# Cross-attention and an eight-expert layer on one core: a new layout of the first two periods, and a new order of ScalarE's and VectorE's work in all of them

## The reference

```
h = layernorm(x)
q = h @ wq;  k = ctx @ wk;  v = ctx @ wv            # 16 heads of 64
x2 = x + softmax(q k^T / 8) v @ wo + bo
g = layernorm(x2)
gates = softmax(g @ router_w + router_b)            # 8 experts, the best 2 are chosen
# each expert takes its first 640 tokens in order of token number
x_out = x2 + sum over chosen e: gate_e * (gelu(g @ w1[e] + b1[e]) @ w2[e] + b2[e])
```

## Time and profile before

| | |
|---|---|
| median of 3 runs | 1056.79 us (1056.28 to 1056.82) |
| the profiled execution's own time | 1054.35 us |
| its span, first to last instruction | 1052.5 us |
| PE, DVE, ACT, POOL busy | 968.4, 774.7, 628.0, 260.1 us |
| mean granted TensorE clock | 0.977 of full speed |

### The profile page before, as it was taken

The page is one execution under the profiler, slowest core; times in us unless marked ns, Lnnn a source line. Parts: engine busy times, 40 slices in busy tenths (PEclk is TensorE's granted clock), DMA queues, the critical chain, the costliest instruction groups (busy, mean ns, idle before and its releaser), DMA issues.

```text
span 1052.5 us, 22859 instructions
## 1 busy us (share of the span) xinstructions
PE 968.4 (92%) x8224; PEld 872.0 (83%) x8224; DVE 774.7 (74%) x2096; ACT 628.0 (60%) x1738; POOL 260.1 (25%) x428
## 2 busy tenths in 40 slices
PE   4789999999999999999999999999845999999996
PEld 3678888888888888888888888888644999999996
DVE  4777778788887878788787878878663667766662
ACT  3777777766776767677766767777522334443330
POOL 2320211223131322313132231301231322222332
PEclk9899999999999999999999999999976999999998
DMA  8530101000010101011010101000024244445522
GB/s 226 149 105 2 32 1 32 22 31 23 31 51 7 39 13 31 13 31 42 2 41 6 31 8 32 16 1 15 12 97 172 60 93 124 125 125 132 132 26 26
DMA packets 47822, 56.73 MB, mean 54 GB/s; under 512 B 5228, under 2 KB 43098, under 8 KB 47584
## 3 DMA queue, kind: packets, MB, share of 16 engines
q1 hardware_dynamic: 38880, 46.30, 14.2%
q0 software_dynamic: 8832, 8.98, 5.3%
HBM read 36.01 MB, written 24.20 MB: 57 GB/s over the span
## 4 chain that ended last, share of the span: by engine, by line
PE 70%; ACT 12%; DVE 8%; issue 6%; DMA 1%; POOL 1%; POOLq 0%; another core or an unknown queue 0%; SPq 0%; ACTq 0%; DVEq 0%
PE psum L494 33%; PE psum L678 11%; PE psum L587 10%; PE psum L557 8%; PE psum L573 7%; ACT prob L739 6%; ACT probt L693 3%; DVE prob L907 3%; ACT kh L693 1%; PE psum L643 1%; DVE kl L844 1%; PE psum L605 1%; DVE negmax L896 1%; DMA slot_table<-row,picki 1%; ACT ah L693 1%
## 5 line engine op out<-in xcount | busy, mean ns | idle before, releaser
L739 ACT ACTIVATE prob<-psum,negmax 128x256 f32<-128x256 f32 x512 | 241.5, 489 | 98.2 <-DVE negmax L896 98.2
L693 ACT ACTIVATE probt<-psum 128x512 f32<-128x512 f32 x256 | 160.1, 631 | 41.2 <-PE psum L573 40.1
L896 DVE TENSOR_REDUCE negmax<-psum 128x2 f32<-128x512 f32 x256 | 159.0, 683 | 22.8 <-PE psum L557 22.4
L907 DVE TENSOR_SCALAR prob<-prob,invtot 128x256 f32<-128x256 f32 x512 | 160.2, 376 | 4.5
L573 PE MATMUL psum<-ident,prob 128*128 128x128 f32 x1024 | 153.2, 273 | 1.8 <-ACT probt L693 1.0
L820 ACT ACTIVATE hid<-psum,b1t 128x640 f32<-128x640 f32 x64 | 50.9, 796 | 136.3 <-PE psum L494 136.3
L573 PEld LDWEIGHTS psum<-ident,prob 128*128 128x128 f32 x1024 | 119.6, 142 | 13.9 <-issue 3.8
L587 PE MATMUL psum<-probt,v 128*64 128x256 f32 x1024 | 126.0, 389 | 0.0
L446 POOL DMA_INDIRECT slot_table<-row,picki x64 | 65.8, 1028 | 198.6 <-DVE picki L1009 171.8
L739 ACT ACTIVATION_READ_ACCUMULATOR prob<-psum,negmax 128x1 f32 x512 | 112.8, 220 | 0.0
L557 PE MATMUL psum<-kh,qh 64*128 64x256 f32 x512 | 84.1, 307 | 30.2 <-ACT probt L693 26.4
(11 more groups left out here) (155 smaller groups left out, 2738.8 us busy)
## 6 DMA issues: line engine op xcount, KB each, us to landing
w1r<-in_w SPq DMA_DIRECT2D x8, 1024.0 KB, 8.1
w2r<-in_w SPq DMA_DIRECT2D x8, 1024.0 KB
slot_table<-blank SPq DMA_DIRECT2D x8, 662.5 KB, 9.7
rows<-slot_table SPq DMA_DIRECT2D x8, 662.5 KB, 5.3
xin<-in_x SPq DMA_DIRECT2D x16, 256.0 KB, 2.9
out_rows<-x SPq DMA_DIRECT2D x16, 256.0 KB, 3.2
c<-in_ctxt SPq DMA_DIRECT2D x16, 128.0 KB, 3.0
c<-in_ctxt SPq DMA_DIRECT2D x32, 64.0 KB, 2.9
```

Source lines behind the costliest of these rows:

```text
L693: copy = lambda dst, src, **kw: act.activation(dst, src, ACT.Copy, **kw)
L739: last = act.activation(prob[:, m % 2, u, qb, :], psum[:, u, qb * S:(qb + 1) * S], ACT.Exp, bias=negmax[:, m % 2, u, qb:qb + 1], accum_out ...
L896: dve.tensor_reduce(negmax[:, m % 2, u, :], psum[:, u, :].rearrange("p (q s) -> p q s", q=ST), AX.X, ALU.max, negate=True).then_inc(sem("m ...
L907: last = dve.tensor_scalar(prob[:, m % 2, u, qb, :], prob[:, m % 2, u, qb, :], invtot[:, m % 2, u, qb:qb + 1], None, ALU.mult)
```

## The change

The first two periods get their own order in `timeline()`, ahead of a loop that now starts at m = 1. TensorE turns the unit matrix 28 times ahead of the first `xt` and 8 times behind it, into a PSUM bank that nobody reads then (`warm`). wq and wk come in two quarters of 256 columns and a half (`SPLITS`); wv and wo come in halves and are split by GpSimd alone (`vsplit`, a cast and a subtraction of 1024 columns). The q of period 1 is made ahead of the scores of period 0. The constants and the sums with the output's bias stand later on GpSimd (`constants` in period 2, `residual` for batches 0 and 1 in period 3), and so does the clearing of the table.

In every period: ScalarE does `exp1` right behind `exp0`, ahead of `pv`'s head; its copy of v (`v_sb`) goes behind the copy of `turn2`. On VectorE the ranks, and the addition that makes x2 from the second half of the output projection (`x2add`), go from the end of r = 0 into r = 1, between `max1` and `max2`.

At the end: w1 and w2 of expert 0 load once q is complete and x2 of batch 13 is stored; ScalarE makes the heads at the end of period 63 (`whi`) and VectorE the rests at four places of the last stages (`wlo`). The weights of expert 1 load ahead of the wait for the last scatter. The first expert's rows come in three DMAs with a semaphore each, and the first half of `up` starts with two groups of rows. In the last batch, two additions to `before` that nobody reads are left out.

```diff
-SPLITS = [(0, 0), (1, 0), (2, 0), (0, 1), (1, 1), (2, 1), (3, 0), (3, 1)]
+SPLITS = [(0, 0, 256), (1, 0, 256), (0, 256, 512), (1, 256, 512), (0, 512, 1024), (1, 512, 1024)]
+VSPLITS = [(2, 0, 512), (2, 512, 1024), (3, 0, 512), (3, 512, 1024)]
...
-    out = [("ln1_stats", 0), ("ctx", 0), ("split", 0), ("ln1", 0), ("split", 1), ("xt", 0), ("q", 0), ("k", 0),
-           ("split", 2), ("split", 3)]
-    for m in range(PERIODS + 1):
+    out = [("ln1_stats", 0), ("ctx", 0), ("ln1", 0), ("split", 0), ("split", 1), ("warm", 0), ("xt", 0), ("warm", 1),
+           ("split", 2), ("split", 3), ("q", 0), ("k", 0), ("q", 1), ("vsplit", 0), ("vsplit", 1), ("hi", 4),
+           ("scores", 0), ("max0", 0), ("max1", 0), ("max2", 0), ("max3", 0), ("exp0", 0), ("k", 1), ("exp1", 0),
+           ("lo", 4), ("exp2", 0), ("exp3", 0), ("v", 0), ("v_sb", 0), ("hi", 5), ("inv0", 0), ("norm0", 0),
+           ("norm1", 0), ("ctx", 1)]
+    for m in range(1, PERIODS + 1):
...
-        out += [("scores", m), ("max0", m), ("max1", m), ("max2", m), ("max3", m), ("exp0", m)] if live else []
+        out += [("scores", m), ("max0", m), ("max1", m), ("exp0", m), ("exp1", m)] if live else []
+        if r == 1 and 3 <= b < B:
+            out += [("rank", b - 3)]
+        if r == 1 and 2 <= b < B:
+            out += [("x2add", ST * (b - 2) + 1)]
+        out += [("lo", 5)] if m == 1 else []
+        out += [("max2", m), ("max3", m)] if live else []
...
-            out += [("ln2_stats", B - 2), *scaled]
+            out += [("ln2_stats", B - 2), *scaled, ("wlo", 0)]
...
-        out += [("exp1", m)] if live else []
...
+        out += [("ln1_stats", 1)] if m == 1 else []
...
-        out += {0: [("split", 4)], 1: [("split", 5)], 2: [("split", 6)], 3: [("split", 7)]}.get(m, [])
...
-            out += {0: [("ln1_stats", 1)], 1: [("ln1", 1)]}.get(r, [])
+            out += {1: [("vsplit", 2), ("ln1", 1)], 2: [("vsplit", 3), ("constants", 0)],
+                    3: [("residual", 0), ("residual", 1)]}.get(r, [])
...
-            out += {0: [("gate", b - 3), ("rank", b - 3)], 3: [("pick", b - 3)]}.get(r, [])
+            out += {0: [("gate", b - 3)], 3: [("pick", b - 3)]}.get(r, [])
...
         out += [("turn2", m - 1)] if turned else []
+        out += [("v_sb", m)] if live else []
...
+            out += [("whi", piece) for piece in range(WSPLITS)]
...
-    out += [("slot", last - 2), ("ln2", last - 1), ("keys", last - 2), ("pick", last - 2),
+    out += [("slot", last - 2), ("ln2", last - 1), ("keys", last - 2), ("pick", last - 2), ("wlo", 1),
...
-            ("gate", last - 1), ("o", ST * B - 2), ("rank", last - 1), ("o", ST * B - 1), ("ln2_stats", last),
-            ("pos", last - 1), ("slot", last - 1), ("keys", last - 1), ("pick", last - 1), ("ln2", last)]
+            ("gate", last - 1), ("wlo", 2), ("o", ST * B - 2), ("x2add", ST * B - 2), ("rank", last - 1), ("o", ST * B - 1),
+            ("x2add", ST * B - 1), ("ln2_stats", last),
+            ("pos", last - 1), ("slot", last - 1), ("keys", last - 1), ("pick", last - 1), ("ln2", last), ("wlo", 3)]
...
             load_x(0)
+            load_split(0)
             load_ctx(0)
...
+            for at in range(1, 4):
+                load_split(at)
+            load_vsplit(0)
+            load_split(4)
+            load_split(5)
             load_x(1)
             load_ctx(1)
...
+            load_vsplit(1)
+            sp.dma_start(bo_all[:, :], bo.partition_broadcast(P)).then_inc(sem("const_in"), 16)
+            load_vsplit(2)
+            load_vsplit(3)
             load_x(2)
             load_x(3)
...
+            load_ctx(2)
             sp.wait_ge(sem("blank"), 1)
...
+                if b == B - 3:
+                    sp.wait_ge(sem("q"), PERIODS)
+                    load_w(0)
...
+            load_w(1)
             sp.wait_ge(sem("scatter"), 16 * 2 * ST * B)
             all_stored(sp)
             load_rows(0)
             sp.dma_start(b2_all[:, :, :], b2.partition_broadcast(P)).then_inc(sem("b2_in"), 16)
             load_rows(1)
-            for e in range(1, NE):
+            load_rows(2)
+            for e in range(2, NE):
...
+                    for u in range(TURNS):
+                        s0, s1 = 2 * u, min(2 * u + 2, ET)
+                        sp.dma_start(rows[:, 0, s0:s1, :],
+                                     table[s0 * P:s1 * P, :].rearrange("(s p) w -> p s w", p=P))\
+                          .then_inc(sem(f"rows_first{u}"), 16)
...
+            def vsplit(w):
+                pool.wait_ge(sem(f"v_in{w}"), 48 if VSPLITS[w][0] == 2 else 16)
+                whole, head, rest_ = vpieces(w)
+                link(pool.tensor_copy(head, whole))
+                pool.tensor_tensor(rest_, whole, head.bitcast(F32), ALU.subtract).then_inc(sem("vsplit"), 1)
...
+            def warm(at):
+                for j in range((28, 8)[at]):
+                    pe.transpose(psum[:, 4, j % 4 * P:(j % 4 + 1) * P], ident[:, :], ident[:, :])
...
-                pe.wait_ge(sem("buf_lo"), TURNS * (e + 1))
+                pe.wait_ge(sem("buf_lo"), TURNS * (e + 1) - (e == 0))
...
+                        if at == 0 and half == 1:
+                            pe.wait_ge(sem("buf_lo"), TURNS)
...
             def keys(b):
                 dve.wait_ge(sem("slots"), b + 1)
-                for t in range(ST):
+                for t in range(ST if b + 1 < B else 0):
```

More of the change, by code:

```diff
@@ L118, in timeline @@
         if m == PERIODS - 1:
-            out += [("gate", b - 2), ("rank", b - 2), ("o", ST * (b - 1) + 1), ("pos", b - 2)]
+            out += [("gate", b - 2), ("rank", b - 2), ("o", ST * (b - 1) + 1), ("x2add", ST * (b - 1) + 1),
+                    ("pos", b - 2)]
+            out += [("whi", piece) for piece in range(WSPLITS)]
         if r == 1 and 3 <= b < B:
@@ L268, in all_stored, with rows_ready @@
                 eng.wait_ge(sem(f"x2_out{r}"), 16 * B // 2)
+        def rows_ready(eng, e, u):
+            if e == 0:
+                eng.wait_ge(sem(f"rows_first{u}"), 16)
+            else:
+                eng.wait_ge(sem(f"rows_in{e % 2}"), 16 * ((e + 1) // 2))
         @block.sync
@@ L457, in _ @@
                     inverse_root(stage[:3], n)
-                if stage == "ln1":
-                    if n == 1 and "c" not in did:
-                        did.add("c")
-                        constants()
-                    ln1(n)
+                if stage == "vsplit":
+                    vsplit(n)
+                if stage == "constants":
+                    constants()
+                if stage == "residual":
+                    residual(n)
                 if stage == "pick":
@@ L535, in v_ @@
                 if n in (0, 2):
-                    pe.wait_ge(sem("split_lo"), 3 if n == 0 else 6)
+                    pe.wait_ge(sem("vsplit"), 1 if n == 0 else 2)
                 cols, tt = slice(half * 512, half * 512 + 512), slice(t * P, (t + 1) * P)
@@ L756, in pv @@
                 if m == PER_B:
-                    act.wait_ge(sem("split_lo"), 8)
+                    act.wait_ge(sem("vsplit"), 4)
                 if b >= 2:
@@ L772, in gate @@
                 act.activation(lexp[:, :, :], logit[:, :, :], ACT.Exp).then_inc(sem("gate_exp"), 1)
-            steps = dict(split=split, xt=xt, q=q, k=k, v=v_, pv=pv, x2t=x2t_, gate=gate,
-                         exp0=lambda m: exps(m, 0), exp1=lambda m: exps(m, 1), exp2=lambda m: exps(m, 2),
-                         exp3=lambda m: exps(m, 3), turn0=lambda m: turn(m, 0), turn1=lambda m: turn(m, 1),
-                         turn2=lambda m: turn(m, 2), turn3=lambda m: turn(m, 3))
-            for stage, n in TIMELINE:
-                if stage in steps:
-                    steps[stage](n)
             def split_w(e, piece):
                 r, part, cut = e % 2, *divmod(piece, WSPLITS // 2)
+                if e == 0:
+                    act.wait_ge(sem(("k", "v")[part]), (PERIODS, 4 * B)[part])
                 act.wait_ge(sem(("w1_in", "w2_in")[part]), 16 * (e + 1))
@@ L793, in split_w @@
                     .then_inc(sem("wsplit_hi"), 1)
+            steps = dict(split=split, hi=split, xt=xt, q=q, k=k, v_sb=v_, pv=pv, x2t=x2t_, gate=gate,
+                         whi=lambda piece: split_w(0, piece),
+                         exp0=lambda m: exps(m, 0), exp1=lambda m: exps(m, 1), exp2=lambda m: exps(m, 2),
+                         exp3=lambda m: exps(m, 3), turn0=lambda m: turn(m, 0), turn1=lambda m: turn(m, 1),
+                         turn2=lambda m: turn(m, 2), turn3=lambda m: turn(m, 3))
+            for stage, n in TIMELINE:
+                if stage in steps:
+                    steps[stage](n)
             def turn_rows(e, u):
@@ L1059, in weigh @@
                                   None, ALU.mult).then_inc(sem("y"), 1)
-            for piece in range(WSPLITS):
-                split_w(0, piece)
             for u in range(TURNS):
```

133 lines of the change are left out of this document (63 added, 70 removed).

## The result

The changed kernel took 1027.17 us (median of 4 runs, 1025.74 to 1029.63) beside 1056.53 of the kernel before: a ratio of 0.9725, 95% interval 0.9705 to 0.9745, 2.7% faster. 1025 was forecast. The profiled execution took 1026.53 us with a span of 1024.8, 27.7 less than the 1052.5 of before; 31.8 had been forecast for it.

The account below looks back on a forecast made before the run. TensorE, busy for 92% of the span, was taken as the bound. Steady periods 14, beginning 14.8 and end 3 sum to 31.8 us, off the profiled 1054.35: 1022.5, plus 2.44 for the median: 1025; range 1014 to 1037.

Parts of the forecast that it names:

- Beginning: Start up to the ninth scores: new order and layout bring them from 109.80 to 95.0, 14.8 us gained, bounds 7 and 20.
- floor of 9.33 a period: Steady periods: TensorE's own work when nothing waits, 9.33 us together; periods 3 to 7 of the start were counted at it.
- Steady periods: From the ninth scores on: reordered VectorE and ScalarE work removes the waits before the scores, 14 us gained, bounds 5 and 16.
- the loss in r=2: Period r=2 of each batch: late exps cost 0.15 us a batch, taken 13 times off the 16.1 us of waits.
- exp1 ahead of `ah` costs nothing: ScalarE in the steady periods: both exps end with the product (3.5 against 3.58 us), so moving exp1 costs nothing.
- r=2 holds 2.87+0.44 more TensorE work, which covers it: Period r=2: exps start 2.7 us behind their scores, and the extra TensorE work of 2.87+0.44 us hides that.
- rival D: Periods with a late second maximum: exp1 ahead of `ah` delays it and q's copy, 51 us, total 1090; chance 0.03.
- End: End of attention up to the experts: scatter, additions, first rows and first product gain 3 us, bounds 0.5 and 4.5.
- priced at -0.5: Splits of expert 0's weights beside the scatter of 758: may cost 1.0 us on the chain, half of it taken.
- E: Start: GpSimd's pieces take 8 us each, table clear at 80, a VectorE copy waits 6 us more: 1031; chance 0.06.
- A: Slow start: port lock or late clock keeps 8 us of the beginning's gain away: 1033; chance 0.18.
- B: Steady waits only shrink, as VectorE is full in r=1: 6 us gained instead of 14, 1033; chance 0.12.

Follow-up runs that it names:

- second profile of the changed kernel: The changed kernel itself run once more, unaltered, in the third group of runs: 1026.65 us, ratio 0.9709 to the kernel before.
- `slot` early: The changed kernel with slot of r=2 between the second and third maximum instead of behind the head of the product: 1019.33 us, ratio 0.9682 to the kernel before.

## Why the prediction was right, point by point

- **Beginning: 14.8 forecast, 15.35 measured.** First scores 14.47 (14.9 forecast), period 1 at 19.29 (19.3), period 2 at 30.03 (31.3), period 3 at 42.83 (42.3), ninth 94.45 (95.0). 11.8 us of it is the layout: the kernel with the three steady edits and the old beginning has its ninth scores at 106.28. The other 3.5 us are v's copy, which the forecast had counted inside the floor of 9.33 a period: with that edit alone, period 3's scores stand where they did (53.66, 53.77 before) and the ninth 3.6 us sooner. Of the layout, only the unit turns were taken out by themselves (2.5 to 3.0 us); the quarters, the early q and GpSimd's splits were not tested one by one. GpSimd's splits cost 3.42 us a piece (1.04 and 2.38), not 4.5, but one of the four took 4.28: its subtraction met VectorE's split of wk and took 3.24. Period 1 lasted 10.7 us (12 forecast) and period 2 12.8 (11): VectorE lost more in period 2 than forecast and less in period 1. No stretch at half clock came (1.7 forecast); in three of the variants with this beginning one of 3.4 us did.
- **Steady periods: 14 forecast, 10.9 measured.** The mechanism was right: idle time ahead of the scores fell from 17.3 to 1.2 us. The gain in r=0, r=1 and r=3 was 16.9 us, where 16.1 had been forecast. The step that failed is the loss in r=2, put at 0.15 us a batch (2.0 in all): it was 6.0. Behind it stand "exp1 ahead of `ah` costs nothing" and "r=2 holds 2.87+0.44 more TensorE work, which covers it". The late start of r=2's exps was forecast (2.7 us behind the scores; 2.6 measured), and so was the rule of rival D: over 1.7 us late, `ah` is held up. I applied it to r=1, where the maxima moved forward, and not to r=2, which I had just made late. There 0.89 us of delay on `ah` went on to al, slot and k, and came out at TensorE as 0.57. The experiments show it three times (12.54 to 13.03 with the edit, 13.12 to 12.54 without, and 12.54 with `slot` out of the way). The covering work stands behind k in the list and could not help.
- **End: 3 forecast, 1.8 measured up to the experts** (1.51 lost, 2.38 and 0.96 gained). Three gains are there by the trace: the scatter took 5.95 us from its first instruction to landing (7.04), the rows 2.79 (4.20), the first product starts 0.96 sooner; only the rows have an experiment. The loss of 1.51 is a stretch of 3.41 us at half clock over the product with v of period 63, which took 3.62 us. In the second profile of the changed kernel it took 1.95, and "late" is 47.24 (timelines of TensorE, the first profile and the second):
```profile
737.79 3.62 PE L637 MATMUL psum<-probt,v 128*64 128x256 f32 x16
```
```profile
738.44 1.95 PE L637 MATMUL psum<-probt,v 128*64 128x256 f32 x16
```
- **What is open in the end.** Whether the new end makes such stretches likelier. "Late" is 47.35 to 47.40 in four of the five profiles with the old end and 49.46 in the fifth; with the new end it is 47.24 and 47.37 in two of nine, and 48.58 to 51.00 in the other seven.
- **Terms of the end that came out otherwise.** `wlo` beside the scatter of batch 12, priced at -0.5, did nothing there: the instructions took 0.97 to 1.11. The cost came at batch 14 instead, where the first scatter instruction took 2.14 (1.08 before). load_w(1), priced at nothing, was issued 3.7 us ahead of the last scatter DMA of that batch, which took 4.80 us to land. The two together held the last batch's scatter by some 0.2 us; they weren't tested apart. The 0.36 saved in `before` does not show: the logits came 0.36 later behind x2's turn, which now lies at half clock. The weights of expert 0 were issued at 710.05; the forecast's 736 was the end of the last q in the kernel before.
- **The sum.** 31.8 was forecast for the span and 27.7 measured, 4.1 less. The forecast median is only 2.2 us off, since the profiled execution of the kernel before stood 2.4 us below its median and that of the changed kernel 0.6: that is luck.
- **Rivals.** E did not come: the table's clearing was issued from 42.91 (44 forecast), and VectorE did not wait. A's 8 us did not come either, though its mechanism did (the 2.54 us of `xn`). B came in a milder form: norms end late in r=1, and r=1 takes 10.03 instead of 9.87 in some profiles. D came, in r=2 alone, and cost 5 to 6 us in place of 51; its sign, `ah` over 0.5 us behind its product, was there (0.89).

## The version that beats both

The changed kernel with `exp1` back: 1019.89 us, ratio 0.9653 to the kernel before, 0.7% less than the changed kernel beside it. `slot` early gives much the same (0.9682); the intervals of the two overlap, and they ran in different groups.

## What to carry to other kernels

When an edit makes one engine's input late on purpose ("the next period covers it"), go through each step queued behind the late instruction on each engine, the PSUM bank that it frees among them; covering work helps only what stands behind it in program order. Of two reorderings that belong together, price each at the periods that the other has changed. In this kernel, work on GpSimd cost VectorE little while GpSimd's instructions were short (0.73 us) or VectorE read PSUM; a long one (2.38) stopped VectorE for up to its own length. Cutting it up made GpSimd itself 1.6 us or more slower a piece, and paid nothing here since VectorE was waiting for GpSimd's next result.

## What the runs showed of the hardware

- One VectorE instruction on SBUF (0.34 to 0.51 us for 256 columns when alone) took 2.54 beside a GpSimd subtraction of 2.38, and one of 1.2 took 3.32; with subtractions of 0.73 none took over 1.23. It goes the other way too: a GpSimd subtraction that began while VectorE's split of wk ran took 3.24. VectorE's reads of PSUM beside the same GpSimd work kept their 0.67 to 0.69. These traces agree with the Trainium skill ("SBUF — State Buffer", section "SBUF: two separate sides"), which calls the port pair of the two engines an exclusive lock. That it would cost 8 us, as rival A had it, they don't show.
- GpSimd's instruction for an indirect DMA (a scatter) took mostly 0.97 to 1.1 us and otherwise at most 1.24. When it began 0.04 to 0.1 us behind the start of a VectorE subtraction with two inputs in SBUF, it took 2.14 (in the changed kernel) and 1.97 (in the kernel before).
- A cast and a subtraction of 1024 columns on GpSimd took 1.04 and 2.38 us, less than four times 0.40 and 0.73.
- TensorE's granted clock went from 1.2 to 2.4 GHz 3.7 to 6.0 us behind its first matmul in the eight profiles that begin with 28 turns in a row. With a sparser start it took 6.3 to 7.4 in five profiles and 12.0 in a sixth.
- At the end of attention, where TensorE waits often, 0, 3.4, 6.8 or 10.2 us were granted at 1.2 GHz in profiles of kernels with the same work there. "Late" went from 47.24 to 51.00 with it, up to 3.8 us of the total.
